# Small PE products regrouped by tile shape, and an order of work moved by tables, in a fused attention and expert-gated layer

## The chip, the cores and the metric

The kernel runs on one core of one Trainium2 chip. The metric is the device time of one execution in microseconds, as the median of several runs. Lower is better.

## What is computed

The input x has 16 batches of 512 tokens with 256 channels. Each token is normalised (xn), and the output is x + attention(xn) + ffn(xn). Cut to what matters:

```python
# attention: 16 query heads of 16 channels, ONE key head and ONE value head
q  = (xn @ Wq.T + bq) * 16 ** -0.5
k, v = split(xn @ Wkv.T + bkv)                  # 16 channels each
qr = q.reshape(16, 16 * 512, 16)                # 8192 query rows per batch
o  = softmax(qr @ k.T) @ v
attn = o(heads merged) @ Wo.T + bo
# ffn on feats = xn: 6 experts, 100 tokens each, rank 16; top 1 gate
gate   = one_hot(argmax(xn @ w_gate))
tokens = einsum('elr,erc->elc', A, B)
p      = softmax(xn . tokens * 256 ** -0.5)     # over the 100 tokens
delta  = ((p[1:] @ (tokens @ wt.T + wt_b)[1:]) + xn) @ wd.T + wd_b
ffn    = xn + log(guard(sum_e gate * exp(delta * scale)))   # guard: 0 -> eps
```

The large part is the attention: per batch 8192 x 512 scores, their row maxima, exponentials and products with V.

## The kernel before

The 16 batches run through one software pipeline whose clock is a counter of **ticks**, 64 per batch (NT = 1024). In tick n three engines each have a regular step:

- PE computes in `ab` (line 387) 128 query rows against all 512 keys. VectorE (DVE) takes the row maxima of it in `mx` (line 882), negated, into M.
- PE computes in `b` (line 394), 44 ticks later (LB), the transposed scores with the maxima folded in as two more rows of the contraction (50 rows), and ScalarE (ACT) evicts them as exponentials in `ex` (line 690). `bd` is the same product in another bank ring, used in the last batch and the tail.
- Every fourth tick `pv` (line 406) multiplies four tiles of exponentials with V and a column of ones. `ot` copies the sum out every 16 ticks, and through DRAM and `on` it comes back normalised.

`ab` and `b` contract 48 and 50 rows, so they run on halves of the array (tiles of 64 rows) and two run at once. `pv` and the gate product `vg` (line 487) use four tiles of 32 columns. All other products use the whole array, but for the transpose of the maxima `mt` (line 537), which gives 64 columns. Ticks go in **pairs**: two `ab` and two `b`, then one other product, in a **gap** between pairs.

The maxima of 32 ticks go through POOL (GpSimd, `ms`, lines 1018 to 1022: scaled, split in two fp16 parts), PE (`mt`), ACT (`mte`) and a DMA (`md`) into the rows 48 and 49 of Q, where `b` reads them.

The small products of a batch are: `q0`, `q1` (line 476), `uk` (465), `vg` (487) and its transpose `vt` (494), which belong to the batch ahead; `s` (501), `p` (509), `a` (516) for the experts' softmax; `d0` to `d3` (529 and 531) for delta; `o0` to `o3` (548) for the output projection. ACT's `vte` copies V and the gate logits out of `vt`'s bank (lines 652, 653). DVE's `gate` (lines 843 to 854) makes the one-hot of the gate out of them in five operations, each of which waits for the one before. POOL's `mask` and a transposing DMA then give the mask that `utm` (line 1010, product UTm) needs before `s`. `guard0` and `guard1` (lines 1033, 1035) replace zeros before the logarithm, `radd` (line 1040) adds it to the residual; `fo0` to `fo3` (line 906) evict the output.

**What sets the order.** Nothing is scheduled on the chip. `slots()` gives each step a slot, in ticks, out of tables (`SLOT` for all batches, `FIRST`, `SECOND`, `LAST_BUT_ONE` and `LAST` for some, `SETUP`, `HALF`, `QUARTER`, `TAIL`), and every engine issues its own steps in the order of their slots. `put("ab", ...)` makes the pairs. `EXTRA` names the ticks of the last batch in which an additional `b` and `bd` are done, so that fewer are left for after it.

**What sets the waits.** PE's outputs live in two rings of banks of 512 columns: `R1`, four banks (pA in the profile), and `R2`, three (pB). `FREED1` and `FREED2` say which product belongs to which ring and whose semaphore frees its bank. A product takes the next bank of its ring and waits for the reader of the product four (pA) or three (pB) turns earlier:

```python
            k = TURN[0][name, key] - N1
            return FREED1[TURNS[0][k][1]](TURNS[0][k][2]) if k >= 0 else (S("id"), 0)
```

At the start `warm0` and `warm1` (line 414) multiply the identity with itself, 56 and 12 times, into pO, where nothing reads it. The first `ab` waits for a DMA that brings Q back from DRAM.

## Time and profile before

| | |
|---|---|
| median of 3 runs | 890.01 us (889.68 to 891.96) |
| the profiled execution, its own time | 891.21 us |
| its span, first to last instruction | 889.4 us |
| mean granted TensorE clock | 0.976 of full speed |
| busy: PE, DVE, ACT, POOL | 94%, 87%, 77%, 64% of the span |
| share of the chain that ended last: PE, DVE, issue, POOL, ACT | 78%, 13%, 3%, 2%, 2% |

The busy share is the time in which an engine worked on anything. PE's matmuls are pipelined, so that one's duration is longer than the distance to the next: distances between starts are what costs time. An operation is named by its line, its output tile and its inputs. Idle time stands in brackets with what ended it. The chain is followed back from the last instruction to what released each step.

### The profile page before, as it was taken

What the parts mean: (1) busy time and instruction counts of PE and PEld (TensorE: products, weight loads), DVE (VectorE), ACT (ScalarE), POOL (GpSimd) and SP (SyncE); (2) the same over time, 40 slices, a digit from 0 to 9 for tenths busy, and PEclk for the clock granted to TensorE, in tenths of its full rate; (3) what the DMA queues carried; (4) which work ended last, traced back from release to release, by engine and by line L of the source; (5) the groups of instructions that cost most, each with busy time, mean ns of one, the idle gap of its engine ahead of it and who ended that gap; (6) DMA issues with size and microseconds to landing.
All of it is one profiled execution on the core that took longest, in us unless ns stands there. A gap on an engine that the chain in (4) does not pass through costs nothing.

```text
span 889.4 us, 18179 instructions
## 1 busy us (share of the span) xinstructions
PE 837.5 (94%) x6040; PEld 278.2 (31%) x6040; DVE 771.1 (87%) x1488; ACT 687.1 (77%) x1388; POOL 567.9 (64%) x760
## 2 busy tenths in 40 slices
PE   6679999999999999999999999999999999999897
PEld 5323223332323333232333323233333323232223
DVE  7688898989989898998989889898989989898756
ACT  2226888788888888888888888888888888888894
POOL 2865677576676767666676776667776666746131
PEclk7687999999999999999999999999999999999999
DMA  4413243435524453442445354344445434341122
GB/s 119 116 36 71 68 103 87 119 86 122 117 81 104 104 124 79 132 104 88 94 112 117 78 139 98 102 90 115 105 106 120 89 115 86 83 104 60 63 64 71
DMA packets 129883, 86.08 MB, mean 97 GB/s; under 512 B 63487, under 2 KB 113920, under 8 KB 129792
## 3 DMA queue, kind: packets, MB, share of 16 engines
q1 hardware_dynamic: 129312, 84.56, 38.8%
q8 instruction: 51, 0.84, 0.4%
q10 hardware_dynamic: 480, 0.36, 0.2%
q14 instruction: 40, 0.33, 0.1%
HBM read 39.30 MB, written 33.54 MB: 82 GB/s over the span
## 4 chain that ended last, share of the span: by engine, by line
PE 78%; DVE 13%; issue 3%; POOL 2%; ACT 2%; DMA 0%; DVEq 0%; POOLq 0%
PE pO L406 25%; PE pA L387 18%; PE pB L394 9%; DVE M L882 7%; PE pA L529 5%; PE pA L476 5%; PE pA L548 4%; PE pA L531 3%; PE pA L465 3%; PE pA L501 2%; PE pA L516 2%; ACT P L690 2%; DVE st L810 1%; PE pB L509 1%; DVE RL L895 1%
## 5 line engine op out<-in xcount | busy, mean ns | idle before, releaser
L882 DVE TENSOR_REDUCE M<-pA 128x1 f32<-128x512 f32 x1024 | 649.9, 679 | 87.0 <-PE pA L387 86.0
L690 ACT ACTIVATE P<-pB 128x512 f32<-128x512 f32 x1002 | 554.9, 604 | 121.6 <-PE pB L394 119.7
L387 PE MATMUL pA<-K,Q 48*128 48x512 f16 x1024 | 321.4, 388 | 28.8 <-DVE M L882 14.4
L394 PE MATMUL pB<-Q,K 50*128 50x512 f16 x1002 | 314.2, 384 | 0.2
L406 PE MATMUL pO<-P,VK 128*32 128x512 f32 x2048 | 272.1, 604 | 0.4 <-ACT P L690 0.2
L387 PEld LDWEIGHTS pA<-K,Q 48*128 48x128 f16 x1024 | 67.8, 94 | 340.5 <-DVE M L882 275.1
L1040 POOL TENSOR_TENSOR Rs<-Rs,Cz 128x512 f32<-128x512 f32 x32 | 40.7, 1271 | 53.2 <-ACT Cz L676 51.0
L406 PEld LDWEIGHTS pO<-P,VK 128*32 128x32 f32 x2048 | 40.6, 108 | 93.7 <-issue 59.5
L394 PEld LDWEIGHTS pB<-Q,K 50*128 50x128 f16 x1002 | 64.4, 94 | 5.1 <-ACT P L690 3.6
L1033 POOL TENSOR_SCALAR Cz<-Cx 128x512 f32<-128x512 f32 x32 | 62.1, 1941 | 3.0 <-ACT Cx L670 3.0
L995 POOL CAST Qp<-qf 128x512 f16<-128x512 f32 x31 | 18.9, 610 | 64.7 <-ACT qf L637 64.6
L529 PE MATMUL pA<-wcP,xT 128*128 128x256 f16 x384 | 54.3, 279 | 0.8 <-DVE M L882 0.7
L548 PE MATMUL pA<-woP,OnP 128*128 128x256 f16 x369 | 51.2, 274 | 0.1
L476 PE MATMUL pA<-xT,wqP 128*128 128x512 f16 x192 | 49.5, 396 | 1.3 <-DVE M L882 0.5
L1018 POOL TENSOR_SCALAR Ms<-M 128x32 f32<-128x32 f32 (+1 forms) x34 | 10.1, 296 | 59.9 <-DVE M L882 59.9
L1048 POOL TENSOR_TENSOR On<-Op,Rb 128x512 f32<-128x512 f32 x31 | 39.8, 1285 | 13.0 <-DMA Rb<-l_parts 10.7
L1027 POOL TENSOR_TENSOR En<-Es,sR 128x400 f32<-128x400 f32 x16 | 13.7, 853 | 50.8 <-DVE sR L869 50.8
L670 ACT ACTIVATE Cx<-pA,sc_d 128x256 f32<-128x256 f32 x64 | 30.8, 482 | 16.2 <-PE pA L531 16.2
L529 PEld LDWEIGHTS pA<-wcP,xT 128*128 128x128 f16 x384 | 32.8, 99 | 31.6 <-DVE M L882 19.8
L1035 POOL TENSOR_TENSOR Cx<-Cx,Cz 128x512 f32<-128x512 f32 x32 | 40.7, 1272 | 2.7
L548 PEld LDWEIGHTS pA<-woP,OnP 128*128 128x128 f16 x369 | 31.1, 98 | 31.2 <-DVE M L882 17.6
L531 PE MATMUL pA<-W,MmT 98*128 98x256 f32 x128 | 39.2, 388 | 0.0
(170 smaller groups left out, 898.1 us busy)
## 6 DMA issues: line engine op xcount, KB each, us to landing
o_parts<-OTr SPq DMA_DIRECT2D x62, 256.0 KB, 2.3
X<-in_x SPq DMA_DIRECT2D x16, 512.0 KB, 3.9
q_pieces<-Qp SPq DMA_DIRECT2D x64, 128.0 KB
out<-OUT SPq DMA_DIRECT2D x32, 256.0 KB, 3.7
Op<-o_parts SPq DMA_DIRECT2D x31, 256.0 KB
Rb<-l_parts SPq DMA_DIRECT2D x31, 256.0 KB
Q<-q_pieces SPq DMA_DIRECT2D x28, 256.0 KB, 4.4
Q<-q_pieces SPq DMA_DIRECT2D x32, 128.0 KB, 4.4
```

The source lines that it names most:

```text
L387: e.matmul(bank1("ab", t)[:, :], rows[r:r + 48, :], K16[r:r + 48, b % 3, :], start=True, stop=True).then_inc(S("a"))
L394: e.matmul(bankB(u)[:, :], K16[r:r + 50, b % 3, 128 * i:128 * i + 128], cols[r:r + 50, :, :], start=True, stop=True).then_inc(S("b"))
L406: mm = e.matmul(pO[32 * j:32 * j + 32, :], VK[:, b % 3, i, :], P[:, p % PR, :], start=(i == 0), stop=(i == 3))
L476: mm = e.matmul(bank1(f"q{g}", b)[:, :], wqP[:, wp, c, 128 * g:128 * g + 128], xT[:, b % 2, :, xp, c, :], start=(k == 0 and c == 0), stop= ...
L529: e.matmul(dst, xT[:, b % 2, t, xp, c, :], wcP[:, wp, c, 0:C], start=(k == 0 and c == 0), stop=False)
L531: e.matmul(dst, MmT[0:ER + 2, 128 * t:128 * t + 128], W2[0:ER + 2, :], start=False, stop=True).then_inc(S("d"))
L548: mm = e.matmul(bankO(t, b), OnP[:, b % 2, part, op, 128 * t:128 * t + 128], woP[:, wp, part, :], start=(part == 0 and k == 0), stop=(part ...
L690: e.activation(P[:, u % PR, :], bankB(u)[:, :], ACT.Exp, scale=alpha).then_inc(S("e"))
L882: e.tensor_reduce(M[:, t // 32 % 2, t % 2, t % 32 // 2:t % 32 // 2 + 1], bank1("ab", t)[:, :], AX, ALU.max, negate=True).then_inc(S("mx"))
L1033: e.tensor_scalar(cz, cx, 0.0, F32_EPS, ALU.is_equal, ALU.mult).then_inc(S("c0"))
L1035: e.tensor_tensor(cx, cx, cz, ALU.add).then_inc(S("c1"))
L1040: e.tensor_tensor(Rs[:, b % 5, 2 * k:2 * k + 2, :], Rs[:, b % 5, 2 * k:2 * k + 2, :], Cz[:, 2 * k:2 * k + 2, :], ALU.add).then_inc(S("r2"))
```

## The change

- `stretch()` replaces the pairs: in each batch but the last, ticks 18 to 20, 21 to 23, 34 to 36, 37 to 39, 50 to 52 and 53 to 55 form stretches of three, and three gaps disappear. Three `pv` move by half a tick or more (`PV_AT`).
- `vg` moves to ring R1 and directly behind a `pv`; `vt` directly behind `q1`; `p` beside `o3`, `d2` into the gap that `vt` had.
- `gate` becomes `gate0` to `gate4` with slots of their own; `vte`, `vge` come earlier with their products.
- M2 gets 64 more columns of zeros, and `mt` transposes all 128.
- The identity products: `warm0` 136 instead of 56, and a new `warm2` of 100 behind the first batch's `vt`.
- First batch: `a`, `d0`, `d1`, `d2` and `guard0` later, `vg` and `vt` of the next batch earlier.
- Last batches: `d2`, `d3` earlier, the output products of the batch three from the end apart, seven `EXTRA` instead of eight.

```diff
-    "kd": -41.6, "vg": -45, "vge": -44.3, "q1": -41, "qe1": -39.4, "qs1": -38.2, "qw1": -35.6,
-    "vt": -37, "vte": -36.4, "gate": -34.8, "mask": -32.6, "mkd": -31.4,
+    "kd": -41.6, "vg": -46.9, "vge": -46.3, "q1": -43.5, "qe1": -41.3, "qs1": -38.2, "qw1": -35.6,
+    "vt": -43.4, "vte": -42.9, "gate0": -36.2, "gate1": -35.2, "gate2": -34.2, "gate3": -33.2, "gate4": -32.7,
+    "mask": -32.2, "mkd": -31.4,
...
-    "d0": 25, "dexp0": 25.6, "d1": 29, "dexp1": 29.6, "guard0": 30.8, "dlog0": 34.2, "radd0": 35.6,
+    "qs1": -50, "vg": -50, "vge": -50.5, "vt": -48, "vte": -47, "gate0": -46, "gate1": -45.9, "gate2": -45.8, "gate3": -45.7, "gate4": -45.6, "mask": -45, "qw1": -40, "mkd": -39,
+    "utm": -30, "s": 9, "smax": 9.6, "sexp": 10.2, "ssum": 10.8, "snorm": 11.4, "p": 17, "pte": 17.6, "a": 23.6, "mm": 24.2,
+    "d0": 29, "dexp0": 29.6, "d1": 31, "dexp1": 31.6, "guard0": 36.6, "dlog0": 40.2, "radd0": 42,
+    "d2": 39, "dexp2": 39.6,
...
+    "d2": 19, "dexp2": 19.6, "d3": 35, "dexp3": 35.6,
...
-EXTRA = (15, 19, 23, 27, 43.4, 51, 59, 63)
-EXTRA_PV = (25.1, 45.1)
+STRETCH = (0, 2, 4, 6, 8, 10, 12, 14, 16, 18, 21, 24, 26, 28, 30, 32, 34, 37, 40, 42, 44, 46, 48, 50, 53, 56, 58, 60, 62)
+PV_AT = {5: 3.5, 9: 3.5, 13: 3.5}
+EXTRA = (15, 23, 31, 39, 47, 55, 63)
+EXTRA_PV = (33.1, 45.1)
...
+    def stretch(n):
+        k = n % 64
+        first = max(m for m in STRETCH if m <= k) if n < NT - 64 else k - k % 2
+        return n - k + first + 0.02 * (k - first)
...
-        put("ab", n - n % 2 + 0.02 * (n % 2), n)
+        put("ab", stretch(n), n)
...
-            places.append((n - n % 2 + 0.02 * (n % 2), "b", n + 0.5))
+            places.append((stretch(n), "b", n + 0.5))
...
-    products = [4 * k + 1 for k in range(LV, NT // 4)] + [last + k for k in EXTRA_PV]
+    products = [4 * k + (PV_AT.get(k % 16, 1) if k < NT // 4 - 16 else 1) for k in range(LV, NT // 4)] + [last + k for k in EXTRA_PV]
...
-        M2 = sb("M2", [128, 2, 2, H], F16)
+        M2 = sb("M2", [128, 128], F16)
...
-            "a": lambda b: (S("mm"), b + 1), "rg": lambda b: (S("two"), 2), "bs": lambda b: (S("scl"), 1),
+            "a": lambda b: (S("mm"), b + 1), "vg": lambda b: (S("vge"), b + 1), "rg": lambda b: (S("two"), 2), "bs": lambda b: (S("scl"), 1),
...
-            "b": lambda u: (S("e"), u + 1), "vg": lambda b: (S("vge"), b + 1),
+            "b": lambda u: (S("e"), u + 1),
...
-                for k, count in enumerate((56, 12)):
+                for k, count in enumerate((136, 12, 100)):
...
-                    w.wait_ge(*before2("vg", b))
+                    w.wait_ge(*before1("vg", b))
...
-                    e.transpose(bank2("mt", g)[:, :].bitcast(F16)[0:64, 0:128],
-                                M2[:, :, :, :].rearrange("p a k h -> p (a k h)"), idh[:, :]).then_inc(S("mt"))
+                    w.wait_ge(S("mz"), 1)
+                    e.transpose(bank2("mt", g)[:, :].bitcast(F16)[:, 0:128], M2[:, :], idh[:, :]).then_inc(S("mt"))
...
-                if (b := due("gate", n)) is not None:
+                if (b := due("gate0", n)) is not None:
                     w.wait_ge(S("gt"), b + 1)
                     e.tensor_reduce(gmx[:, :], G[:, :, :], AX, ALU.max).then_inc(S("g0"))
+
+                if (b := due("gate1", n)) is not None:
...
+            e.memset(M2[:, 64:128], 0.0).then_inc(S("mz"))
...
```

What the order becomes, at three places. In these rows Q16 and K16 are the operands of `ab` (pA) and `b` (pB), and the digit behind pA or pB is the bank.

PE, ticks 16 to 22 of a middle batch, with the gate product `vg`. Before:

```order
L387 MATMUL pA0<-K16,Q16 128x512
L394 MATMUL pB0<-Q16,K16 128x512
L387 MATMUL pA1<-K16,Q16 128x512
L394 MATMUL pB1<-Q16,K16 128x512
L487 MATMUL pB2<-xT,wcP 32x128 x24
L387 MATMUL pA2<-K16,Q16 128x512
L394 MATMUL pB0<-Q16,K16 128x512
L387 MATMUL pA3<-K16,Q16 128x512
L394 MATMUL pB1<-Q16,K16 128x512
L406 MATMUL pO<-P,VK 32x512 x4
```

and `vt` stood alone in its gap three pairs later:

```order
L387 MATMUL pA2<-K16,Q16 128x512
L394 MATMUL pB1<-Q16,K16 128x512
L494 MATMUL pB2<-idf,VGs 128x128
L387 MATMUL pA3<-K16,Q16 128x512
L394 MATMUL pB0<-Q16,K16 128x512
```

Changed:

```order
L423 MATMUL pO<-P,VK 32x512 x4
L504 MATMUL pA3<-xT,wcP 32x128 x24
L404 MATMUL pA0<-K16,Q16 128x512
L411 MATMUL pB2<-Q16,K16 128x512
L404 MATMUL pA1<-K16,Q16 128x512
L411 MATMUL pB0<-Q16,K16 128x512
L404 MATMUL pA2<-K16,Q16 128x512
L411 MATMUL pB1<-Q16,K16 128x512
L493 MATMUL pA3<-xT,wqP 128x512 x6
L511 MATMUL pB2<-idf,VGs 128x128
L404 MATMUL pA0<-K16,Q16 128x512
L411 MATMUL pB0<-Q16,K16 128x512
```

`vg` (x24) has left its own gap and pB for a place behind `pv` in pA3, three ticks follow it in one stretch, and the transpose `vt` follows the six passes of `q1` without a pair between them.

DVE, ticks 27 to 31 of the same batch (M is the row maxima, L843 to L854 and L860 to L879 the gate). Before:

```order
L882 TENSOR_REDUCE M<-pA3 128x1
L816 BN_AGGR mv<-st 128x2 x4
L882 TENSOR_REDUCE M<-pA0 128x1
L843 TENSOR_REDUCE gmx<-G 128x4
L845 TENSOR_TENSOR geq<-G,gmx 128x24
L848 TENSOR_TENSOR gw<-geq,prio 128x24
L851 TENSOR_REDUCE gm2<-gw 128x4
L854 TENSOR_TENSOR oh<-gw,gm2 128x24
L882 TENSOR_REDUCE M<-pA1 128x1
L882 TENSOR_REDUCE M<-pA2 128x1
L882 TENSOR_REDUCE M<-pA3 128x1
L906 SCALAR_TENSOR_TENSOR OUT<-pA0,scl,Rs 128x256
```

Changed:

```order
L907 TENSOR_REDUCE M<-pA0 128x1
L860 TENSOR_REDUCE gmx<-G 128x4
L833 BN_AGGR mv<-st 128x2 x4
L907 TENSOR_REDUCE M<-pA2 128x1
L864 TENSOR_TENSOR geq<-G,gmx 128x24
L907 TENSOR_REDUCE M<-pA3 128x1
L869 TENSOR_TENSOR gw<-geq,prio 128x24
L907 TENSOR_REDUCE M<-pA0 128x1
L874 TENSOR_REDUCE gm2<-gw 128x4
L879 TENSOR_TENSOR oh<-gw,gm2 128x24
L907 TENSOR_REDUCE M<-pA1 128x1
L931 SCALAR_TENSOR_TENSOR OUT<-pA2,scl,Rs 128x256
```

The five gate operations stood in one block behind one maximum; now four maxima stand between them and only the last two follow each other.

POOL, first batch, behind the next batch's reciprocal root. Before (the next row is UTm, L1010):

```order
L1033 TENSOR_SCALAR Cz<-Cx 128x512
L1035 TENSOR_TENSOR Cx<-Cx,Cz 128x512
L1003 CAST mk<-oh 128x4x96
L1018 TENSOR_SCALAR Ms<-M 128x32
L1020 CAST M<-Ms 128x2x16
L1022 TENSOR_TENSOR M<-Ms,M 128x2x16
L940 TENSOR_SCALAR nmu<-mv 128x4
L943 TENSOR_SCALAR rbig<-rstd 128x4
L944 TENSOR_SCALAR rone<-rstd 128x4
L945 TENSOR_TENSOR roff<-nmu,rstd 128x4
L950 TENSOR_SCALAR XN<-X,nmu,rbig 128x256 x4
L1040 TENSOR_TENSOR Rs<-Rs,Cz 128x512
```

Changed (the next row is the addition to Rs):

```order
L1029 CAST mk<-oh 128x4x96
L1044 TENSOR_SCALAR Ms<-M 128x32
L1046 CAST M<-Ms 128x2x16
L1048 TENSOR_TENSOR M<-Ms,M 128x2x16
L966 TENSOR_SCALAR nmu<-mv 128x4
L969 TENSOR_SCALAR rbig<-rstd 128x4
L970 TENSOR_SCALAR rone<-rstd 128x4
L971 TENSOR_TENSOR roff<-nmu,rstd 128x4
L976 TENSOR_SCALAR XN<-X,nmu,rbig 128x256 x4
L1059 TENSOR_SCALAR Cz<-Cx 128x512
L1061 TENSOR_TENSOR Cx<-Cx,Cz 128x512
L1036 TENSOR_TENSOR UTm<-UK,mkT 96x512
```

The two guard operations (Cz, Cx) have moved from ahead of the maxima's scaling (Ms, M) to behind the normalisation (XN), where they stand ahead of UTm; the addition to Rs has moved behind UTm.

## Rows read from the trace of the kernel before

**Rows 1.** Stages (us); busy PE, PEld, DVE, ACT, POOL; clock; DMA.

```profile
86.50:806.60 720.10, 701.23 (x5180) 223.78 (x5178) 647.37 (x1222) 597.08 (x1205) 488.90 (x640) 1.00 0.42 102
806.60:858.10 51.50, 45.83 (x337) 13.68 (x336) 41.31 (x70) 44.40 (x91) 21.44 (x29) 1.00 0.16 54
858.10:889.40 31.30, 25.67 (x169) 9.38 (x169) 15.89 (x27) 17.89 (x37) 7.56 (x10) 0.98 0.23 75
```

**Rows 2.** The same view, for stretches by granted clock.

```profile
7.60:11.00 3.40, 0.30 (x5) 0.13 (x2) 2.56 (x13) 0.41 (x2) 2.12 (x7) 1.00 0.87 233
11.00:21.30 10.30, 7.79 (x34) 4.96 (x35) 8.48 (x37) 2.69 (x5) 1.10 (x3) 0.50 0.13 35
28.10:45.10 17.00, 13.56 (x40) 6.19 (x40) 13.19 (x26) 2.98 (x6) 13.85 (x18) 0.50 0.54 120
62.20:75.90 13.70, 11.27 (x43) 5.41 (x45) 9.81 (x18) 4.21 (x9) 8.44 (x17) 0.50 0.42 69
```

**Rows 3.** Timeline of PE: start, length (us), operation; undisturbed places.

```profile
402.18 1.07 PE L406 MATMUL pO<-P,VK 128*32 128x512 f32 x8
403.18 0.39 PE L387 MATMUL pA<-K,Q 48*128 48x512 f16 x1
...
403.72 1.47 PE L476 MATMUL pA<-xT,wqP 128*128 128x512 f16 x6
...
826.05 1.92 PE L406 MATMUL pO<-P,VK 128*32 128x512 f32 x16
```

**Rows 4.** Timeline of PE around `vg`, `vt` and `o1` of one batch.

```profile
410.16 0.39 PE L387 MATMUL pA<-K,Q 48*128 48x512 f16 x1
...
410.89 0.52 PE L487 MATMUL pB<-xT,wcP 128*32 128x128 f16 x24
411.47 0.37 PE L387 MATMUL pA<-K,Q 48*128 48x512 f16 x1
...
412.27 1.06 PE L406 MATMUL pO<-P,VK 128*32 128x512 f32 x8
...
418.06 0.37 PE L387 MATMUL pA<-K,Q 48*128 48x512 f16 x1 [0.25 <-DVE M L882]
...
420.40 0.83 PE L548 MATMUL pA<-woP,OnP 128*128 128x256 f16 x6
421.46 0.39 PE L387 MATMUL pA<-K,Q 48*128 48x512 f16 x1 [0.23 <-DVE M L882]
...
422.38 1.06 PE L406 MATMUL pO<-P,VK 128*32 128x512 f32 x8
```

**Rows 5.** Timeline of ACT and DVE at the same places.

```profile
409.58 0.77 ACT L629 ACTIVATE UK<-pA,ukb,uks 128x512 f32<-128x512 f32 x1
...
419.75 0.17 DVE L843 TENSOR_REDUCE gmx<-G 128x4 f32<-128x24 f32 x1
...
420.72 1.88 DVE L882 TENSOR_REDUCE M<-pA 128x1 f32<-128x512 f32 x3
```

**Rows 6.** Timelines of PE and of POOL, start and first batch.

```profile
1.91 6.00 PE L414 MATMUL pO<-idh 128*128 128x128 f16 x56 [1.91 <-POOL idh L917]
...
30.53 1.03 PE L387 MATMUL pA<-K,Q 48*128 48x512 f16 x4 [5.25 <-DMA Q<-q_pieces]
...
63.86 0.31 PE L537 MATMUL pB<-idh,M 128*64 128x128 f16 x1 [2.93 <-POOL M L1022]
...
59.19 1.94 POOL L1033 TENSOR_SCALAR Cz<-Cx 128x512 f32<-128x512 f32 x1
...
66.88 1.26 POOL L1040 TENSOR_TENSOR Rs<-Rs,Cz 128x512 f32<-128x512 f32 x1
68.10 1.15 POOL L1010 TENSOR_TENSOR UTm<-UK,mkT 96x512 f32<-96x512 f32 x1
```

**Rows 7.** Groups by line, 806.6 to 858.1: busy us, mean ns, idle before, releaser.

```profile
L882 DVE TENSOR_REDUCE M<-pA 128x1 f32<-128x512 f32 x64 | 40.9, 682 | 10.2 <-PE pA L387 9.9
```

**Rows 8.** Groups by line, the whole span, weight loads of the output products.

```profile
L548 PEld LDWEIGHTS pA<-woP,OnP 128*128 128x128 f16 x369 | 31.1, 98 | 31.2 <-DVE M L882 17.6
```

More of the change, by code:

```diff
@@ L96 @@
 DVE_NAMES = ("rngq", "rng", "two", "scl", "wl", "scd", "stats0", "stats1", "stats2", "stats3", "aggr", "refine", "xl0", "xl1",
-             "qs0", "gate", "smax", "ssum", "mm", "mx", "rec", "fo0", "fo1", "fo2",
+             "qs0", "gate0", "gate1", "gate2", "gate3", "gate4", "smax", "ssum", "mm", "mx", "rec", "fo0", "fo1", "fo2",
              "fo3", "nl00", "nl01", "nl02", "nl03", "nl10", "nl11", "nl12", "nl13")
@@ L643, in _ @@
                     w.wait_ge(S("vt"), b)
-                    e.activation(VGs[:, :], bank2("vg", b)[:, 0:128], ACT.Identity,
+                    e.activation(VGs[:, :], bank1("vg", b)[:, 0:128], ACT.Identity,
                                  scale=vsc[:, 0:1], bias=vgb[:, 0:1]).then_inc(S("vge"))
@@ L1014, in _ @@
                     p, hs = (g % 2, slice(0, H)) if q < 0 else (q // 2, slice(8 * (q % 2), 8 * (q % 2) + 8))
-                    m2 = [M2[:, :, k, :] if q < 0 else M2q[:, :, q % 2, k, :] for k in range(2)]
+                    m2 = [M2v[:, :, k, :] if q < 0 else M2q[:, :, q % 2, k, :] for k in range(2)]
                     w.wait_ge(S("mx"), 32 * g + 32 if q < 0 else NT - 64 + 16 * q + 16)
```

22 lines of the change are left out of this document (14 added, 8 removed), and 8 rows, old and new, of tables (SETUP, SLOT).

## Prediction

> **What bounds the kernel now.** I read the busy times by stage first [rows 1]. From 86.5 to 806.6 us PE is busy 701 of 720 us and DVE 647 (90%), so PE sets the pace and DVE is close behind: what PE gives up, DVE can only partly follow. In the last batch (806.6 to 858.1) PE is busy only 45.8 of 51.5 us, DVE 41.3 and ACT 44.4: waits are in there. The third row, the tail, has 37 ACT operations in 17.9 us, 0.48 us each. Then the granted clock at the start [rows 2]: three stretches at 0.50, which is 1.2 GHz, where PE had idled or waited before them; from 75.9 us on it is 2.4 GHz. Then PE's timeline. A pair of ticks costs 0.54 us (403.18 to 403.72) and a pV product of 8 passes 1.00 us (402.18 to 403.18); two in a row are 1.92 us long where one is 1.07 [rows 3], so the second costs 0.85, and the 0.15 us missing is what entering or leaving a shape of tile costs. I take 0.12 us per switch; a batch has 32 gaps in its pairs, so 64 switches.
>
> Last, the waits that repeat in every batch [rows 4]. The pair before the gate product (410.16) takes 0.73 us instead of 0.54, the one after it (411.47 to 412.27) 0.80. The same two numbers stand around the transpose of V and gate, with 0.25 us of waiting before 418.06. The output product at 420.40 is followed by its pair only 1.06 us later, and that pair takes 0.92 us. The cause is on ACT and DVE. ACT evicts a 0.77 us tile between two exponentials, so a pB bank comes late; and the five gate operations on DVE wait for one another for 0.97 us (419.75 to 420.72), so that the row maxima behind them, 0.60 us apart (three in 1.88) and 0.68 us long, free their pA banks late [rows 5].
>
> **The middle batches.** The change removes, per batch: 0.19 + 0.26 us around the gate product (now in a pA bank), the same around the transpose and its 0.25 us (now behind q1), 0.52 + 0.38 - 0.22 us, say 0.68 us, around the first output product (the gate operations now stand singly between maxima, as the second place of the order shows), and 0.27 us behind the p product, which is the pattern of 411.47 again. Together 2.1 us. Three gaps of 32 disappear (gate product behind pV, transpose behind q1, p beside o3), 6 switches, 0.7 us. The widened M transpose has its neighbours' shape: two per batch, one switch each, 0.24 us. Gross 3.0 us. The same columns are streamed as before, the transpose's too.
>
> What comes instead, with the ring rule (pA has 4 turns, pB 3) and the durations of [rows 4, 5]. A product waits for the reader of the turn 4 (or 3) before it, about 0.1 us after that reader ends. In a stretch of three, exponentials start 0.46 us after the first pair product and then 0.48 apart.
> - Ticks 21 to 23: the third b product wants the bank of the transpose, which ACT still copies: about 0.4 us.
> - Tick 24 wants q1's bank. Its eviction stands in ACT's order behind two exponentials: about 0.3 us.
> - Ticks 32 to 39: two stretches of three put six maxima (3.6 us) into 3.3 us of PE work. DVE also carries an OUT operation before and one between. Followed turn by turn: o2 waits 0.3, the stretch behind it 0.5, the rest 0.1.
> - p wants the bank of its stretch's first b product: that exponential ends 0.46 + 0.60 us after the start, the stretch's PE work at 0.77. With the release 0.4 us.
>
> Together 2.0 us. **Net 1.0 us per batch**, and 14 batches make 14 us. The bounds of the net: the new waits may be as large as twice my figure less the slack that DVE has (0.1 x 51 us = 5 us a batch), which I put at a loss of 0.5; and if DVE and ACT catch up in that slack the gain is 2.2. I take the value of the turn-by-turn reading, since the durations in it repeat to 0.01 us.
>
> **The last batch.** PE waits where extra b products stand in neighbouring gaps without a small product. DVE stood idle for 10.2 us in it [rows 7], so with 41.3 us of busy time it could follow a stage 10 us shorter. The change alternates extras and small products: o1, d2, o2, d3, o3 each get a gap between two extras. In the trace four ticks with an extra between two product gaps take about 2.75 us, four ticks with an extra beside another about 3.5. Three or four of the latter become the former, and I take 4.0 us off (between 0 and 6). One extra fewer leaves two exponentials to the tail, where ACT is the bound: 2 x 0.48 = 1.0 us back. **Net 3 us.**
>
> **The first batch.** Four pieces.
> - Identity products. 56 of them took 6.00 us [rows 6], 0.107 each, at 1.2 GHz. With 136, about 53 run so until the clock rises at 7.6 us [rows 2]; the other 83 at half that time end near 12.1 us, just as the range's maxima arrive. PE then comes to the next products at 2.4 instead of 1.2 GHz; in 11.0 to 21.3 PE was busy 7.8 us at the low level [rows 2] while much of the chain is DVE's. I take 0.8 us (0 to 1.5).
> - The second 100 fill PE's idle 5.25 us before 30.53, where it waits for Q's transfer [rows 6]: 100 x 0.053 = 5.3 us, no delay if the clock is up. The reward is in 28.1 to 45.1: PE 13.6 us busy at the low level, but DVE 13.2 of 17.0 [rows 2], so at most 3.8 us. Long rows of maxima leave PE idle again and the clock may fall again: 1.5 us (0 to 3).
> - The guard. POOL ran it (1.94 + 1.26 us from 59.19) before the maxima's scaling, and PE waited 2.93 us for it before 63.86 [rows 6]. That wait goes. But what is late next is POOL itself: the guard now stands ahead of UTm (68.10), which tick 43's s product needs. Only the 1.26 us addition at 66.88 moves behind UTm. So of 2.9 us, 1.3 stay.
> - The low clock of 62.2 to 75.9: DVE 9.8 of 13.7 us, so at most 3.9; the cause, few products per tick, remains: 0.4 us.
>
> **Net 4 us** (0 to 9).
>
> On the identity products the Trainium skill speaks against the change: "TensorE: Matmul & The Clock Gate", Back-to-back issue gap, gives about 81 ns per product of 128 columns in a stream with weight loads. By it the 83 and the 100 would take 2.3 and 2.8 us longer, and the sum would be 5 us higher. No row here shows such a stream at 2.4 GHz; my 0.053 is half of a measured 0.107.
> On the switches its page "TensorEngine Tiling (Array Packing)", Key Properties, says that changing the tiling mode drains the engine. If 128 x 100 counted as another mode than 128 x 128, p beside o3 would save nothing, 0.24 us a batch.
>
> **The sum.** 14 + 3 + 4 = 21 us off the profiled execution's 891.2 gives 870.2. The median of the runs before is 890.0, 1.2 less, so I say 869.0.
>
> **The rivals.**
> - The rings eat it: the waits in the long stretches are 0.8 us per batch more than I read. For it: DVE at 90%. Against: it has slack outside ticks 16 to 40. 14 - 11 leaves 3; 890 - 3 - 7 = 880.
> - More slack than I read: DVE and ACT catch up, 2.2 us per batch, 31 + 7 = 38 us, 852 to 857. For it: new waits of 0.1 to 0.4 us shift the next reader's start as well. Against: six maxima in 3.3 us.
> - The identity products are paced by weight loads: 98 ns each in the row of line 548 [rows 8]. 183 x 0.045 = 8 us too much, 877.
> - Slower: ACT's order. q1's eviction behind two exponentials holds tick 24's bank, and if every stretch of three meets such a late ACT reader, each of six costs 0.6 us. Against a gross 3.0 that is 3.6 plus the 0.3 at tick 24: 0.9 us lost a batch, 13 us, less 7 elsewhere: 896. It decides from 0.5 us lost per batch. Against it: between stretches there is 1.0 us of pV product.
> - Nothing happens: the waits removed reappear exactly, as PE was covering for DVE all along. 887 to 892. Against it: DVE waits for PE in between.
>
> **The numbers.** Forecast 0.55 (862 to 876), rings 0.16, more slack 0.12, weight loads 0.08, slower 0.05, nothing 0.04. The range 857 to 882 leaves out slower, nothing and most of more slack. A measurement of this kernel tells about 0.3% (2.7 us) from no change: faster 0.91, same 0.04, slower 0.05.
>
> **What would show it.** Middle batches of about 50.4 us instead of 51.4; the gates spread on DVE, 0.54 and 0.76 us around the first output product; waits of PE in ticks 23, 24 and 35 to 39 and before p; the gate product directly behind pV in 0.44 us; an M transpose without the 0.12 us; the s product near 67 us, waiting for UTm. The last batch near 48 us, with two more exponentials behind it. If the batches take 51 us or more, the ring reading is wrong; if the first row maximum comes later than 31.5 us, the identity products are.

## The result

The changed kernel takes 873.9 us (median of 4 runs, 873.0 to 874.5) beside 889.9 us before (4 runs, 889.7 to 892.0): ratio 0.981, interval 0.980 to 0.982. It is 16.0 us faster. The forecast was 869.0 us, 21 us faster, with a range of 857 to 882.

| | before | after |
|---|---|---|
| the profiled execution, its own time | 891.2 us | 873.0 us |
| its span | 889.4 us | 871.2 us |
| mean granted TensorE clock | 0.976 | 0.983 |
| busy PE, DVE, ACT, POOL (share of the span) | 94, 87, 77, 64% | 95, 88, 79, 65% |

Where the 18.2 us of span went is read from DVE's row maxima, of which there is one in every tick in both kernels: the start of the first, of the 65th, of the 961st and of the last bound five stages. (The stages that [rows 1] call last batch and tail are the last two here.)

| stage (us) | before | after | difference | forecast |
|---|---|---|---|---|
| start, to the first maximum | 31.17 | 30.54 | -0.6 | first batch |
| first batch | 56.91 | 55.97 | -0.9 | -4 with the start |
| 14 middle batches | 718.97 | 700.48 | -18.5 | -14 |
| last batch | 51.50 | 50.07 | -1.4 | -4 |
| tail, from the last maximum | 30.86 | 34.17 | +3.3 | +1 |

A middle batch went from 51.36 to 50.03 us, which is 1.32 us where 1.0 was forecast. The start, the first and the last batch gave 3.0 us and the tail took 3.3, so that the two ends together cost 0.3 us where 7 were to be won.

The busy times by stage, which answer to [rows 1] (same columns), and then the stretches by granted clock, which answer to [rows 2]:

```profile
86.50:786.50 700.00, 679.68 (x5168) 223.40 (x5166) 640.00 (x1220) 594.50 (x1202) 490.79 (x639) 1.00 0.42 105
786.50:837.40 50.90, 46.02 (x341) 14.24 (x340) 42.20 (x71) 44.56 (x91) 22.28 (x29) 1.00 0.17 55
837.40:871.20 33.80, 25.28 (x167) 9.04 (x165) 13.79 (x26) 17.95 (x37) 6.80 (x9) 0.98 0.22 69
...
33.40:43.60 10.20, 9.92 (x32) 5.65 (x32) 7.56 (x14) 1.80 (x4) 7.55 (x8) 0.50 0.74 154
64.10:74.40 10.30, 8.76 (x35) 4.33 (x34) 7.79 (x14) 3.90 (x8) 6.49 (x6) 0.50 0.48 79
```

PE is now busy 97.1% of the middle stretch (679.7 of 700.0) and DVE 91.4%. It was 97.4% and 89.9% of the longer one before. PE did not get fuller: its work got shorter, and the waits stayed about as large a share as before. The tail is longer though PE and DVE have a little less to do in it than in [rows 1]: it is waits. At the start one low stretch of the clock (11.0 to 21.3 us) is gone, in the first batch a new one has come at 53.9, and the two others are shorter by 6.8 and 3.4 us.

The ends have to be read with care, because they differ between executions of the same code. Four of the kernels below (the changed one, the eighth extra, the later `sl0`, the old last batch) have the same start and first batch: the first maximum comes at 30.54, 31.16, 32.00 and 31.40 us, and the 65th at 86.51, 87.59, 86.63 and 87.42. So 1.1 us of the 65th maximum is no effect of an edit. Their middle batches agree to 0.01 us.

**A middle batch.** PE's timeline around the gate product, the transpose of V and gate, tick 24, the first output product, a transpose of the maxima and `p`; it answers to [rows 3, 4]:

```profile
399.62 1.06 PE L423 MATMUL pO<-P,VK 128*32 128x512 f32 x8
400.50 0.52 PE L504 MATMUL pA<-xT,wcP 128*32 128x128 f16 x24
400.95 0.39 PE L404 MATMUL pA<-K,Q 48*128 48x512 f16 x1
...
401.76 1.47 PE L493 MATMUL pA<-xT,wqP 128*128 128x512 f16 x6
403.07 0.27 PE L511 MATMUL pB<-idf,VGs 128*128 128x128 f32 x1
403.27 0.39 PE L404 MATMUL pA<-K,Q 48*128 48x512 f16 x1
...
404.13 1.06 PE L423 MATMUL pO<-P,VK 128*32 128x512 f32 x8
405.54 0.39 PE L404 MATMUL pA<-K,Q 48*128 48x512 f16 x1 [0.34 <-ACT qf L654]
...
410.88 0.83 PE L565 MATMUL pA<-woP,OnP 128*128 128x256 f16 x6
411.65 0.39 PE L404 MATMUL pA<-K,Q 48*128 48x512 f16 x1
...
412.43 1.06 PE L423 MATMUL pO<-P,VK 128*32 128x512 f32 x8 [0.18 <-ACT P L707]
...
415.12 0.37 PE L404 MATMUL pA<-K,Q 48*128 48x512 f16 x1
...
416.01 0.37 PE L404 MATMUL pA<-K,Q 48*128 48x512 f16 x1 [0.50 <-DVE M L907]
...
416.55 1.07 PE L423 MATMUL pO<-P,VK 128*32 128x512 f32 x8
...
425.54 0.39 PE L404 MATMUL pA<-K,Q 48*128 48x512 f16 x1
...
426.65 0.64 PE L526 MATMUL pB<-idf,En 128*100 128x128 f32 x4 [0.28 <-ACT P L707]
427.13 0.82 PE L565 MATMUL pA<-woP,OnP 128*128 128x256 f16 x6
```

Read the distance from one start to the next, since the lengths of two products overlap. A pV product alone takes 1.00; here the next product behind it, the gate product, starts after 0.88, so 0.12 us of switching lay there. The gate product costs 0.45 and has hardly a wait around it. q1 takes 1.31 and the transpose behind it 0.20. The output product is followed by its pair after 0.77 instead of 1.06, and p, with o3 directly behind it, takes 0.48.

The new waits show in the same way. The pV product at 404.13 should end at 405.13 and the next pair starts at 405.54: 0.41 us in tick 24. A pair of 0.54 takes 0.78 behind o1. A stretch of three ticks without waits is 0.76 long; behind the transpose of the maxima it takes 1.43 (415.12 to 416.55), before p 1.11 (425.54 to 426.65), behind the transpose of V 0.86 (403.27 to 404.13), and 0.81 in front of q1 (400.95 to 401.76). With some 0.1 between the transpose of the maxima and the stretch behind it that is 1.9 us of new waits.

Two more places of the kernel before, PE again, are needed for comparison:

```profile
417.48 0.33 PE L494 MATMUL pB<-idf,VGs 128*128 128x128 f32 x1
...
436.66 0.64 PE L509 MATMUL pB<-idf,En 128*100 128x128 f32 x4
```

There the transpose of V and gate took 0.58 us to its pair at 418.06 (0.25 of it the wait of [rows 4]), and p 0.66 to its pair at 437.32, which itself took 0.81.

The timeline of ACT there, which answers to [rows 5]:

```profile
403.73 1.09 ACT L707 ACTIVATE P<-pB 128x512 f32<-128x512 f32 x2
...
404.70 0.78 ACT L654 ACTIVATE qf<-pA,bq_s,scl 128x512 f32<-128x512 f32 x1
```

q1's eviction begins 0.97 us after the first of the two exponentials ahead of it and ends at 405.48; tick 24 starts 0.06 us later. On DVE the five gate operations now lie over 2.7 us (409.22 to 411.92), maxima between them, and no longer over 0.97 in one piece.

### The profile page after: what moved, and what is told of

Its sections match the earlier page's. It is cut to its first block, busy times and chain, and to the rows that moved or that the text cites. A ratio compares the mean times of both kernels' runs of the same rounds, so it can differ in the third digit from the quotient of the medians.

```text
span 871.2 us, 18526 instructions
## 1 busy us (share of the span) xinstructions
PE 824.0 (95%) x6220; PEld 286.9 (33%) x6220; DVE 764.0 (88%) x1488; ACT 686.1 (79%) x1388; POOL 570.6 (65%) x761
## 4 chain that ended last, share of the span: by engine, by line
PE 72%; DVE 16%; issue 4%; ACT 4%; POOL 3%; DMA 1%; DVEq 0%; POOLq 0%
PE pO L423 23%; PE pA L404 17%; DVE M L907 9%; PE pB L411 9%; PE pA L493 5%; PE pA L546 5%; PE pA L565 3%; PE pA L548 3%; PE pA L482 2%; ACT P L707 2%; PE pA L518 2%; PE pA L533 2%; DVE st L827 1%; PE pB L526 1%; ACT qf L654 1%
## 5 line engine op out<-in xcount | busy, mean ns | idle before, releaser
L404 PE MATMUL pA<-K,Q 48*128 48x512 f16 x1024 | 309.7, 386 | 21.7 <-DVE M L907 11.4
L411 PE MATMUL pB<-Q,K 50*128 50x512 f16 x1002 | 302.0, 383 | 2.8 <-DVE RL L920 2.6
L1021 POOL CAST Qp<-qf 128x512 f16<-128x512 f32 x31 | 18.9, 611 | 33.5 <-ACT qf L654 33.4
```

Source lines behind the costliest of these rows:

```text
L404: e.matmul(bank1("ab", t)[:, :], rows[r:r + 48, :], K16[r:r + 48, b % 3, :], start=True, stop=True).then_inc(S("a"))
L411: e.matmul(bankB(u)[:, :], K16[r:r + 50, b % 3, 128 * i:128 * i + 128], cols[r:r + 50, :, :], start=True, stop=True).then_inc(S("b"))
```

## The experiments

Five kernels ask about the middle batches, three about the last batch and the tail, two about the start, two join what won. The base of the timed ones is before at 890.7 us (13 runs) or 890.6 (9 runs). The untimed ones (blocked gates, narrow transpose, p in the pA ring, guard earlier, later `sl0`) were executed once, and their times stand against the 873.0 of the changed kernel's profiled execution. One execution can lie 1 to 3 us off by its start, first batch and tail alone, so what an edit did is read from its stage. The stages are those of the table above; PE's groups are read as there.

### Middle batches: which part of the 1.32 us

**The gate operations alone**, in the kernel before:

```diff
-    "gate": -34.8, "mask": -32.6
+    "gate0": -35.2, "gate1": -34.2, "gate2": -33.2, "gate3": -32.4, "gate4": -31.4, "mask": -31.3
```

> The kernel before, with one part of the change alone: the five gate operations stand singly between row maxima on DVE. My theory (each removed wait is worth what the replay said): o1 and its pair take 0.76 + 0.6 us instead of 1.06 + 0.92, so the middle batch falls from 51.44 to about 50.8 us and the span by 9 us. Rival (DVE at 90% is the real bound, so that waits only move): the period stays above 51.3 us and the span falls by less than 2 us. The last batch and the tail stay as in the kernel before.

890.9 us (10 runs) against 890.7: ratio 1.000, interval 0.999 to 1.001. A middle batch takes 51.32 instead of 51.36. PE's timeline of this kernel at the output products (`mt` is line 537 here):

```profile
422.21 1.06 PE L406 MATMUL pO<-P,VK 128*32 128x512 f32 x8 [0.18 <-ACT P L690]
...
424.92 0.22 PE L537 MATMUL pB<-idh,M 128*64 128x128 f16 x1 [0.33 <-POOL M L1030]
```

At o1 the output product (from 420.67) takes the 0.76 us expected, but its pair 0.78 (421.43 to 422.21) and not the 0.6 expected, as in the changed kernel: 0.44 us are won there. At the next output product, at 423.75, they are lost again: the transpose of the maxima follows it after 1.17 us instead of 0.76 and waits for POOL's M. POOL's timeline shows why M is late:

```profile
423.40 0.50 POOL L1011 CAST mk<-oh 128x384 bf16<-128x384 f32 x1 [1.89 <-DVE oh L862]
423.87 0.29 POOL L1026 TENSOR_SCALAR Ms<-M 128x32 f32<-128x32 f32 x1
```

The mask (mk) stands in POOL's order ahead of the scaling of the maxima (Ms). It needs the last gate operation, which this edit puts at tick -31.4, and waits 1.89 us for it. In the kernel before it did not wait, and the scaling started at 422.69, 1.2 us earlier. The number is the rival's, but its reason, that DVE is the real bound, is not shown by it: the wait came back through a slot of this very edit. The changed kernel has its last gate operation at -32.7, and there the mask waits 0.16 us. What the changed kernel's own slots for the gate would be worth in the old kernel was not run.

**The gate operations in one block again**, in the changed kernel:

```diff
-    "gate0": -36.2, "gate1": -35.2, "gate2": -34.2, "gate3": -33.2, "gate4": -32.7,
+    "gate0": -34.8, "gate1": -34.78, "gate2": -34.76, "gate3": -34.74, "gate4": -34.72,
```

> The changed kernel with the five gate operations back in one block behind the maximum of tick 28, all else as changed. Alone in the kernel before, spreading them gave 0.06 us a batch, because the wait came back at o2 and the M transpose. Theory now (DVE bounds ticks 19 to 40 in the changed kernel, where d2's gap was taken away, so every 0.1 us of DVE there counts): the block, 0.97 us against 0.5 us spread, makes the middle batch 0.3 to 0.6 us longer than 50.08. Rival (spreading is worth nothing here either; the gain is all from gaps and switches): at most 0.1 us longer.

877.4 us beside 873.0, and a middle batch of 50.34 instead of 50.03: 0.31 us, within the 0.3 to 0.6 of the theory. Its timeline of PE:

```profile
412.30 0.39 PE L404 MATMUL pA<-K,Q 48*128 48x512 f16 x1
...
416.90 0.37 PE L404 MATMUL pA<-K,Q 48*128 48x512 f16 x1 [0.60 <-DVE M L907]
```

From the output product, at 411.42, to its pair it is 0.88 us (0.77 with the gates apart), the pair takes 0.92 (0.78), the stretch behind it 0.86 (0.76), and the wait behind the maxima's transpose is 0.60 (0.50). So with all else changed the spread is worth 0.31 us a batch, under half of the 0.68 of the forecast. This is not to be set beside the 0.04 of the kernel before as the same edit in two places, since the slots of the gate and of the mask are others.

**The maxima's transpose to 64 columns again:**

```diff
-    e.transpose(bank2("mt", g)[:, :].bitcast(F16)[:, 0:128], M2[:, :], idh[:, :])
+    e.transpose(bank2("mt", g)[:, :].bitcast(F16)[0:64, 0:128], M2[:, 0:64], idh[:, :])
```

> The changed kernel with the transpose of the maxima back at 64 columns. Theory (each change of tile shape costs PE about 0.1 us, and d, o and the widened transpose share one): the d product before it goes from 1.10 back to 1.19 us and the transpose from 0.15 to 0.18, twice a batch: 0.12 us where PE is the bound (behind d1), nothing where the stretch behind o2 waits for DVE anyway, so 50.15 to 50.25 us. Rival (a switch hides behind the weight loads and costs nothing): 50.08 us.

877.3 us, and a middle batch of 50.25: 0.21 us longer, at two transposes a batch. That is the upper end of the 50.15 to 50.25 expected; only one of the two was expected to count, and both do. PE's timeline of this kernel:

```profile
390.15 0.83 PE L546 MATMUL pA<-wcP,xT 128*128 128x256 f16 x6
...
391.34 0.24 PE L555 MATMUL pB<-idh,M 128*64 128x128 f16 x1
391.52 0.39 PE L404 MATMUL pA<-K,Q 48*128 48x512 f16 x1
```

The delta product in front takes 1.19 us with the narrow transpose behind it, the transpose 0.18. At the same place of the changed kernel they start at 388.01 and 389.11 and the pair at 389.26: 1.10 and 0.15. Nothing but the shape of the transpose differs: 0.12 us for each.

**q1's eviction earlier:**

```diff
-    "qe1": -41.3
+    "qe1": -42.7
```

> The changed kernel with the eviction of q1 moved on ACT ahead of the exponentials of ticks 21 and 22. Theory (tick 24 waits 0.40 us for this eviction alone): the wait goes, but the exponentials behind it come 0.66 us later and give back up to half: period 50.08 to between 49.7 and 49.9 us, span 3 to 5 us shorter. Rival (ACT's total work before tick 24 is what counts, whatever its order): the wait moves to the b product of tick 24, period 50.0 to 50.2 us, no change that can be measured.

872.0 us (871.7 to 872.6), ratio 0.980 (0.978 to 0.981); a middle batch of 49.86, 0.17 us shorter, as the theory had it. Its timeline of PE:

```profile
402.32 1.07 PE L423 MATMUL pO<-P,VK 128*32 128x512 f32 x8
403.32 0.39 PE L404 MATMUL pA<-K,Q 48*128 48x512 f16 x1
...
404.05 1.07 PE L423 MATMUL pO<-P,VK 128*32 128x512 f32 x8
```

The pV product takes its 1.00 us again, so the 0.41 us of tick 24 were the wait for q1's bank, whose eviction now begins at 401.74. But the pair that follows takes 0.73 instead of 0.54; on ACT the exponentials ahead of it now stand behind the eviction. Of 0.41 us, 0.17 are kept.

**p in the pA ring** (three lines: `FREED2` to `FREED1`, `before2` to `before1`, `bank2` to `bank1`):

> The changed kernel with the p product in the ring of four banks. Theory (p waits 0.35 us for the exponential of the first tick of its own stretch, the ring of three being too short): p follows its stretch at once (0.76 us after its start instead of 1.11), the stretch behind o3 may wait 0.1 to 0.2 us for a maximum instead: period 49.8 to 50.0 us. Rival (the wait moves in full to the stretch of tick 53, since DVE has to do six maxima there): 50.05 to 50.1 us.

873.8 us, and a middle batch of 50.00, 0.04 us shorter (the whole is no shorter, because the tail of this execution takes 36.16 us; more on that below). Its timeline of PE:

```profile
424.56 0.39 PE L404 MATMUL pA<-K,Q 48*128 48x512 f16 x1
...
425.31 0.65 PE L526 MATMUL pA<-idf,En 128*100 128x128 f32 x4
425.90 0.83 PE L565 MATMUL pA<-woP,OnP 128*128 128x256 f16 x6
```

The stretch before p takes 0.75 (1.11 in the changed kernel), so p waited for the bank of that stretch's own exponential. But p itself now takes 0.59 (0.48) and the stretch behind o3 0.97 (426.66 to 427.63; 0.76 without waits): an extra turn of the pA ring has to be freed by DVE or by ACT's copy, and 0.3 of the 0.36 us come back there. The 50.00 is the edge of the theory's range and the wait moved nearly in full, as the rival has it.

### Last batch and tail

**An eighth extra tick:**

```diff
-EXTRA = (15, 23, 31, 39, 47, 55, 63)
+EXTRA = (15, 23, 31, 39, 47, 55, 59, 63)
```

> The changed kernel with an eighth extra pair of b products in the last batch, at its tick 59. Theory (the last two b products wait for the reciprocals of the denominators, 2.56 us, because their pB turn comes behind sl0): with them done earlier that wait goes, the tail falls from 34.2 to about 31.0 us, the last batch grows by 0.3 to 0.5: 2.7 us faster than the changed kernel. Rival (the tail is only ACT's count of exponentials, 0.48 us each): 0.5 us faster at most. Middle batches unchanged at 50.08 us.

870.5 us (869.5 to 870.9), ratio 0.977 (0.976 to 0.979): 3.5 us less than the changed kernel, and more than the theory asked. The last batch takes 50.59 us (+0.5) and the tail 30.44 (-3.7). In the changed kernel's tail, PE's timeline shows why:

```profile
857.55 0.39 PE L411 MATMUL pB<-Q,K 50*128 50x512 f16 x1 [2.56 <-DVE RL L920]
```

`sl0` (line 575) gathers the sums into one pB bank, and DVE works through that bank in four reciprocals with a product between them, from 852.73 on. The last one begins at 856.56 and ends at 857.50, and 0.05 us later the b product that needs the bank starts. Meanwhile ACT has nothing to do for 2.9 us. With the eighth extra the last b product is the one that follows `sl0` directly, at 853.75 us in that kernel, and it does not wait.

**sl0 later, the exponentials kept in the tail:**

```diff
-    "sl0": 86.4
+    "sl0": 92.6
```

> The changed kernel with sl0, the product of the denominators, moved on PE from ahead of the last two pairs of b products to behind the last of them; nothing else. Theory (the last b product waits 2.6 to 3.9 us only because its pB turn follows sl0): the wait for the reciprocals goes although the number of exponentials in the tail stays at 30; the reciprocals start about 3 us later and the chain behind them with them, so the tail is 32 to 34 us instead of 34.2 to 36.6. Rival (the tail is long because two more exponentials and a late output product fill it): 34 us and more.

871.4 us beside 873.0; the tail takes 32.56 us instead of 34.17. The last b product starts at 853.75 and `sl0` behind it at 854.07: no product waits for the reciprocals, with all 30 exponentials in the tail. Of the 3.3 us that the tail had grown, 1.6 went with this wait alone.

It is worth more in other executions. The changed kernel and the six others with its extras and its `sl0` all have this wait, 2.5 to 3.9 us long, and none of the rest has it. Two of the seven (the changed one and the narrow transpose) take 34.2 us for the tail. The other five take 35.5 to 36.7, and in exactly those the granted clock is at its low level for 3.4 to 6.8 us around or behind this wait, as in the kernel with the guard earlier, whose PE waits until 860.87 us (the third number from the end is the clock):

```profile
860.00:866.80 6.80, 5.93 (x23) 1.46 (x24) 1.50 (x4) 1.67 (x3) 0.00 (x0) 0.50 0.11 39
```

So where PE idled, the clock could fall as well and the wait cost a second time; with the same order of the tail it did so in five profiles and not in two.

**The last batch as before, in the changed kernel:**

```diff
-    "d2": 19, "dexp2": 19.6, "d3": 35, "dexp3": 35.6,
+    "d2": 39, "dexp2": 39.6, "d3": 47, "dexp3": 47.6,
...
-    "o1": 139, "fo1": 139.6, "o2": 155, "fo2": 155.6, "o3": 179, "fo3": 179.6,
+    "o1": 159, "fo1": 159.6, "o2": 163, "fo2": 163.6, "o3": 183, "fo3": 183.6,
...
-QUARTER_LAST = {4 * NB - 5: 4, 4 * NB - 4: 8, 4 * NB - 3: 12, 4 * NB - 2: 12, 4 * NB - 1: 12}
+QUARTER_LAST = {4 * NB - 6: 4, 4 * NB - 5: 4, 4 * NB - 4: 8, 4 * NB - 3: 12, 4 * NB - 2: 12, 4 * NB - 1: 12}
...
-EXTRA = (15, 23, 31, 39, 47, 55, 63)
-EXTRA_PV = (33.1, 45.1)
+EXTRA = (15, 19, 23, 27, 43.4, 51, 59, 63)
+EXTRA_PV = (25.1, 45.1)
```

> The changed kernel with the last batch as it was before: eight extras at their old ticks, d2 and d3, the output products of the batch three from the end and the copies of pO as before. Theory (the change to the last batch was a loss: 1.4 us gained in it, 3.3 us lost behind it): middle batches 50.03, last batch 51.5, tail 30.9, span 869.3, some 2 us faster than the changed kernel. Rival (the shorter middle batches bring POOL and the DMAs late in the tail, whatever the last batch looks like): tail 33 us or more, no gain over the changed kernel.

872.0 us (871.4 to 872.1), ratio 0.979 (0.977 to 0.980): 1.9 us less than the changed kernel, whose highest and lowest runs (874.5, 873.0) lie above all of these. The last batch takes 51.38 us (+1.3), the tail 31.11 (-3.1). This part of the change was a loss as a whole. The kernel with the eighth extra parts it in two: it has the new order with eight extras, and takes 50.59 us for the last batch and 30.44 for the tail. So the new order alone won 0.8 us in the batch and cost the tail nothing; the one extra fewer won 0.5 and cost 3.7.

Why it gained so little where 4 were forecast shows in PE's timeline of the changed kernel's last batch, in a group with an extra:

```profile
797.10 0.39 PE L404 MATMUL pA<-K,Q 48*128 48x512 f16 x1
...
798.30 0.37 PE L404 MATMUL pA<-K,Q 48*128 48x512 f16 x1 [0.37 <-DVE M L907]
...
799.28 0.37 PE L404 MATMUL pA<-K,Q 48*128 48x512 f16 x1 [0.59 <-ACT P L707]
799.60 1.06 PE L423 MATMUL pO<-P,VK 128*32 128x512 f32 x8
```

And the one extra of the kernel before that stood alone between two gaps with small products:

```profile
840.52 0.39 PE L387 MATMUL pA<-K,Q 48*128 48x512 f16 x1
...
842.70 0.37 PE L387 MATMUL pA<-K,Q 48*128 48x512 f16 x1 [0.59 <-ACT P L690]
...
843.02 1.92 PE L406 MATMUL pO<-P,VK 128*32 128x512 f32 x16
```

The four ticks with the extra in their midst take 2.50 us in both (797.10 to 799.60, 840.52 to 843.02) and hold the same two waits, one for DVE and one for ACT. Where extras stood one behind the other, before, they took 2.50 or 2.01 us as well. So an extra was not cheaper for standing alone. Before, five of these groups take 2.50 us and two 2.01; now it is three and three. What makes the difference between 2.50 and 2.01 was not tried.

DVE's idle time from the first maximum of the batch to the last fell from 9.8 to 8.4 us, which is the 1.4 us of the batch.

### Start and first batch

**The guard earlier:**

```diff
-    "guard0": 36.6
+    "guard0": 32.2
```

> The changed kernel with the first batch's guard back ahead of the scaling of the maxima. Theory (POOL's chain up to UTm is the bound between ticks 32 and 43, whichever order it has): PE waits about 2.5 us for the maxima before the M transpose, but only little for UTm, and the s product starts within 0.5 us of 67.96. Rival (the later guard is what gained in the first batch): s and all behind it come 2 us or more later. The first batch is then 0 to 0.5 or 2 us and more longer than 55.97.

878.4 us beside 873.0; the first batch takes 58.62 instead of 55.97. PE's timeline of this kernel:

```profile
65.16 0.26 PE L555 MATMUL pB<-idh,M 128*128 128x128 f16 x1 [3.16 <-issue]
...
69.96 2.03 PE L518 MATMUL pA<-As_s,UTm 96*128 96x100 f32 x8 [0.15 <-DVE M L907]
```

And the same places of the changed kernel, on PE and then on POOL, which answer to [rows 6]:

```profile
23.48 5.75 PE L431 MATMUL pO<-idh 128*128 128x128 f16 x100
30.11 0.61 PE L404 MATMUL pA<-K,Q 48*128 48x512 f16 x4 [0.89 <-DMA Q<-q_pieces]
...
67.96 2.00 PE L518 MATMUL pA<-As_s,UTm 96*128 96x100 f32 x8 [1.54 <-POOL UTm L1036]
```

```profile
66.66 1.15 POOL L1036 TENSOR_TENSOR UTm<-UK,mkT 96x512 f32<-96x512 f32 x1
```

With the guard early, PE waits 3.16 us before the maxima's transpose, much as the 2.9 of [rows 6], and the s product comes at 69.96 us. With the later guard the transpose comes at 61.42 without a wait, UTm at 66.66 instead of 68.16, and s at 67.96, waiting 1.54 us for UTm as forecast. In these two kernels the later guard is worth 2.0 us at the s product and 2.65 over the batch, which is the rival's side.

But this is more than the change gained over the kernel before, for two reasons. The addition to Rs stays behind UTm in both. And the delta products are later than before, so that the guard, moved early alone, waits for its input. POOL's timeline of the kernel with the early guard, and the end of the reciprocal root (rstd) in the changed kernel and in the one before:

```profile
60.89 1.95 POOL L1059 TENSOR_SCALAR Cz<-Cx 128x512 f32<-128x512 f32 x1 [0.96 <-ACT Cx L687]
```

```profile
58.78 0.20 POOL L962 TENSOR_TENSOR rstd<-y 128x4 f32<-128x4 f32 x1
```

```profile
59.03 0.20 POOL L936 TENSOR_TENSOR rstd<-y 128x4 f32<-128x4 f32 x1
```

From the root to UTm, POOL takes 9.07 us before (59.03 to 68.10) and 7.88 changed (58.78 to 66.66): 1.19 us less, which is the 1.26 us addition. With the guard early it is 8.88 (59.28 to 68.16), and the 1.0 us that it is longer than changed is the wait of 0.96 us for ACT's Cx, which the kernel before did not have.

**The identity products as before** (56 and 12, none behind them):

```diff
-                for k, count in enumerate((136, 12, 100)):
+                for k, count in enumerate((56, 12)):
```

> The changed kernel with the old identity products (56 and 12, none behind the first transpose of V and gate). Theory (they are worth little because the start is bound by DMA and DVE): first maximum at 31.2 instead of 30.5 us, and the first batch 1 us longer through a low clock from 28 us on: together 1 to 2 us slower than the changed kernel. Rival (the clock is what the first batch hangs on): 3 us or more slower. Middle batches stay at 50.08 us.

874.8 us (874.4 to 875.0), ratio 0.982 (0.981 to 0.984), beside the changed kernel's 0.981 (0.980 to 0.982): 0.8 us, which the two intervals do not part, and less than the 1 to 2 us of the theory. The start takes 30.87 us instead of 30.54, the first batch 55.98 instead of 55.97: 0.3 us, less than the 1.1 by which the same code differs. The chip's clock is at its low level from 9.6 to 19.9 and from 26.7 to 43.8 us in this kernel, and from 33.4 to 43.6 in the changed one; in six other kernels with the changed one's identity products also for 3.4 to 6.8 us between 16.6 and 23.4. The mean granted clock is 0.971 to 0.973 in all four runs here and 0.982 to 0.983 in the changed kernel's. So the products do lift the clock, and it is worth nearly nothing: the DMAs that bring Q back are issued at 25.98 us here and at 25.95 in the changed kernel, and the first `ab`, and with it the first row maximum, waits for them.

### What won, joined

**The eighth extra, q1's early eviction and p in the pA ring together:**

> The changed kernel with three amendments together: eighth extra pair at tick 59 of the last batch, q1's eviction ahead of the exponentials of ticks 21 and 22, p in the ring of four. If the gains add (3.3 and more for the tail, 2.5 for q1 in the middle batches, 0.5 for p): middle batches 49.83, 866.5 to 868 us median. Rival (waits move among them, as they did when the gates were spread alone): middle batches 49.9 or more and 869 us or more.

866.9 us (5 runs, 865.8 to 868.6), ratio 0.974, interval 0.972 to 0.975. It beats both kernels: 7.0 us under the changed one, 23.6 under before. The middle batch takes 49.83 us, the last 50.60, the tail 31.12. The busy times of its middle stretch:

```profile
86.50:785.30 698.80, 686.33 (x5181) 225.19 (x5181) 640.19 (x1222) 592.78 (x1205) 492.88 (x643) 1.00 0.43 106
```

PE is busy 98.2% of the middle now (686.3 of 698.8).

**The same with q1's eviction at -42 instead of -42.7:**

> As the joined kernel, but q1's eviction between the exponentials of ticks 21 and 22, not ahead of both. Theory (ahead of both, it made the b product of tick 24 wait 0.19 us for the exponential of tick 21; between them that exponential is in time and the bank of q1 still comes only 0.1 us late): 0.05 to 0.1 us a batch less than the joined kernel, 1 us in all. Rival (it is even, a wait of 0.1 to 0.2 us for the one or the other): no difference that can be measured.

868.2 us (867.2 to 869.7), ratio 0.975 (0.973 to 0.976); a middle batch of 49.95 where the joined kernel has 49.83. The medians of the two are not parted, but the middle batches are: the place between wins nothing, and 0.12 of the 0.17 us that the eviction gave are lost. That is neither theory's case.

## Why the prediction was right and where it was wrong

The direction, the size and the main mechanism held, and the 873.9 us lie in the range. The forecast was 4.9 us too low: the middle gave 4.5 us more than I said (18.5 for 14), the ends 7.3 less (a loss of 0.3 for a gain of 7). The two errors partly cancel and leave 2.8, so that the total is nearer than its parts, and that is luck. The other 2.1 are that the median lies 0.9 us above its profiled execution, where I had taken 1.2 below, as before.

**Middle batches, net 1.0 a batch; measured 1.32.** The new waits were forecast at 2.0 us and are 1.9, for the most part where I put them. Tick 24 waits 0.41 (0.3) and for the reason given, which the early eviction shows by removing it; p 0.35 (0.4), also for the reason given, which p in the other ring shows. The transpose's bank costs only 0.10 (0.4). Ticks 32 to 39 cost 1.0 us in all (0.9), though not at o2 (0.3 forecast, nothing measured) but at the pair behind o1 (0.24) and around the maxima's transpose (some 0.75).

The gross gain can be added up from the starts in both timelines. The waits that were there before and are gone are 0.45 us around the gate product, 0.71 around the transpose of V and gate, 0.67 around o1 and 0.27 behind p: 2.10, as forecast. The switches are worth 0.65 (0.7): pV before the gate product 1.00 to 0.88, the gate product 0.58 to 0.45, q1 1.40 to 1.31, the transpose without its wait 0.33 to 0.20, p 0.66 to 0.48. The wide transpose of the maxima measures 0.21 (0.24). What the forecast did not have is that **a third tick in a stretch is cheaper than half a pair**: 0.22 us (0.76 less 0.54) against 0.27. Six stretches of 0.76 in the place of nine pairs of 0.54 are 0.30 us. Together that is 3.3 us, less 1.9, or 1.3 to 1.4.

**What a wait is worth is less than its length.** In the forecast I added the 0.68 us around the first output product like the others, and as a reading of the rows that holds. But putting the gate operations back in one block costs only 0.31. In the same way the 0.41 us of tick 24 are worth 0.17 when they are taken away, and the 0.36 in front of p 0.04: the rest comes back at the next product that needs the same reader. So of the 1.32 us only the 0.31 of the gate and the 0.21 of the transpose are each shown by taking the edit out. The gate product, its transpose, p and the stretches were not taken out one by one; what stands on them is the addition of the rows.

**Last batch, -4; measured -1.4.** The failed step is "three or four of the latter become the former": the groups with an extra did not get shorter by it, because their waits (0.37 for DVE, 0.59 for ACT) are inside them, and the one that already stood alone took 2.50 us as well. The step also does not give its own sum: three or four times 0.75 us are 2.3 to 3.0, not 4.0.

**Tail, +1.0; measured +3.3.** I counted two exponentials more. That count was right and is not what cost most. What was late was a b product whose turn of the pB ring lies behind `sl0`'s bank, which DVE holds through four reciprocals. The row stood in neither of my views, because before that product came earlier than the bank. Moving `sl0` takes 1.6 us of it away; one more extra takes all. The 1.7 us that remain with `sl0` moved hold the two exponentials and a wait of about 1.1 us for POOL's normalised product, before the output product of line 565 (at 843.15 in the changed kernel); they were not taken apart.

**Start and first batch, -4; measured -1.6.** The guard's piece was right in its mechanism and its size: 1.3 forecast, 1.19 us less on POOL from the root to UTm. The two sets of identity products were put at 2.3 us, and the profiles give 0.3. Their step failed where I said that PE at 2.4 instead of 1.2 GHz would bring the start forward: the chain there ends in Q's transfer. For the 0.4 us of the last low stretch I named few products per tick as the cause of the low clock; no run shows that. 1.2 and 0.3 make up the 1.6, but at a spread of 1.1 us in the same code this agreement may be luck. The joined kernel has its 65th maximum at 84.70 us, 1.8 earlier than the changed one, though only q1's eviction and p's bank differ there. The low stretches of the clock lie elsewhere too (in the joined kernel 32.0 to 42.2, 52.5 to 59.3, 62.7 to 66.1 and 69.5 to 73.0 us); whether as cause was not tried.

**The rivals.** "The rings eat it" is what happened in single places (tick 24, p), not in the sum. "More slack" is refuted at 2.2 us a batch, though the joined kernel reaches 1.53. "Paced by weight loads" at 98 ns is refuted: the 100 identity products took 5.75 us, 57 ns each, at the full clock. "Nothing happens" is refuted by 16 us; the gates spread alone in the old kernel gave nothing, but through a slot of that edit (the mask on POOL). "Slower by ACT's order" is refuted: one stretch, not six, meets the late eviction.

The 57 ns speak against the 81 ns that the Trainium skill gives in "TensorE: Matmul & The Clock Gate", Back-to-back issue gap, for such products in a stream. On p beside o3, the 0.48 us against 0.66 for a p between pairs say that 128 x 100 is not another mode than 128 x 128: the draining that the Trainium skill's "TensorEngine Tiling (Array Packing)", Key Properties, describes shows in these rows only between tiles of different rows or columns: 64 rows, 32 or 64 columns, and the whole array.

## What to carry to other kernels

A wait that is seen in a timeline is not a price that can be added up: in the changed kernel the spread of the gate operations is worth 0.31 us of the 0.68 that they had cost, and two waits of 0.41 and 0.36 gave 0.17 and 0.04 when they were taken away. Ask what the same reader, or the queue behind it, holds next; an operation put later on one engine can hold another engine's queue, as the mask did on POOL. Where a stage is shortened by moving work into the next one, look for what else holds the next stage's buffers, not at the count of moved operations. Small products are best placed behind a product of their own tile shape. And before a difference of 1 us at the start or the end is explained, look at how far profiles with the same code there lie apart.
